# A fused attention and feed-forward layer on one core: where the first stage loads, rounds and stores its weights

## What is computed

```python
xn = _layernorm(x)
q, k, v = xn @ Wq.T, xn @ Wk.T, xn @ Wv.T          # 16 heads of 32
probs = softmax(where(causal, q @ k.T / sqrt(32), min))
attn = (probs @ v) @ Wo.T
gate = silu(xn @ f8(gate_w) * gate_scale)          # 512 x 1536
up = xn @ f8(up_w) * up_scale                      # 512 x 1536
ffn = ((gate * up) @ f8(down_w)) * down_scale      # 1536 x 512
```

## Time and profile before

| | |
|---|---|
| median of 3 runs | 1294.6 us (1293.05 to 1294.61) |
| the profiled execution: time, span | 1293.41 us, 1291.6 us |
| PE busy | 1229.4 us (95%) |
| DVE, ACT, POOL busy | 79%, 71%, 68% |
| granted PE clock, mean | 0.992 |
| end of the first stage | 289.1 us |

### The profile page before, as it was taken

The page is one execution under the profiler, slowest core; times in us unless marked ns, Lnnn a source line. Parts: engine busy times, 40 slices in busy tenths (PEclk is TensorE's granted clock), DMA queues, the critical chain, the costliest instruction groups (busy, mean ns, idle before and its releaser), DMA issues.

```text
span 1291.6 us, 32678 instructions
## 1 busy us (share of the span) xinstructions
PE 1229.4 (95%) x11852; PEld 829.0 (64%) x11852; DVE 1021.0 (79%) x2587; ACT 912.7 (71%) x1555; POOL 877.8 (68%) x1033
## 2 busy tenths in 40 slices
PE   4999888898999999999999999999999999999988
PEld 3444334346777777676767677777777677777763
DVE  7878757677878788888888787878888888878762
ACT  3433333328878788888888788878888888888870
POOL 1323323306777787787888788879788788888882
PEclk9999989998999999999999999999999999999999
DMA  8698999578666465757566576756575866667655
GB/s 257 162 243 246 223 232 269 160 226 213 141 115 143 103 145 97 160 114 164 116 141 131 134 153 133 147 124 156 104 169 115 161 116 151 123 139 152 119 110 130
DMA packets 428463, 201.32 MB, mean 156 GB/s; under 512 B 339344, under 2 KB 396688, under 8 KB 427792
## 3 DMA queue, kind: packets, MB, share of 16 engines
q1 hardware_dynamic: 409312, 179.32, 63.8%
q10 hardware_dynamic: 18992, 19.93, 5.7%
HBM read 76.03 MB, written 44.30 MB: 93 GB/s over the span
## 4 chain that ended last, share of the span: by engine, by line
PE 40%; POOL 15%; ACT 7%; DVE 5%; issue 5%; DMA 4%; SPq 1%; ACTq 0%
PE bank L1650 12%; PE bank L1664 10%; POOL row L1318 7%; PE bank L1626 6%; DMA p_t<-row 4%; PE pair L1588 3%; PE pair L233 3%; POOL fuse L1300 3%; POOL probs L1151 3%; ACT probs L1375 2%; PE pair L1602 2%; PE pair L1672 2%; DVE row_top L1528 2%; ACT fuse L1420 1%; POOL p L1312 1%
## 5 line engine op out<-in xcount | busy, mean ns | idle before, releaser
L1385 ACT ACTIVATE p<-pair,s_exp 128x512 f32<-128x512 f32 (+1 forms) x384 | 243.6, 635 | 147.5 <-PE pair L1588 140.3
L1318 POOL TENSOR_TENSOR row<-row 128x896 f16<-128x896 f32 (+1 forms) x128 | 256.4, 2014 | 9.6 <-ACT row L1399 9.6
L1375 ACT CAST probs<-p 128x512 f16<-128x512 f32 (+1 forms) x384 | 214.8, 559 | 14.3 <-POOL p L1312 12.2
L1151 POOL TENSOR_TENSOR probs<-p,probs 128x512 f16<-128x512 f32 x192 | 221.5, 1157 | 0.2
L1650 PE MATMUL bank<-shared,wg 128*128 128x256 f16 x1536 | 200.0, 273 | 0.0
L1650 PE MATMUL bank<-shared,wu 128*128 128x256 f16 x1536 | 200.0, 273 | 0.0
L1664 PE MATMUL bank<-wd,fuse 128*128 128x512 f16 x768 | 190.6, 378 | 0.8 <-DVE ff_out L1509 0.8
L1528 DVE TENSOR_REDUCE row_top<-pair 128x1 f32<-128x896 f32 (+1 forms) x128 | 147.6, 1153 | 36.6 <-PE pair L1606 36.3
L1312 POOL TENSOR_SCALAR_AFFINE_SELECT p<-p 128x128 f32<-128x128 f32 (+1 forms) x256 | 107.6, 425 | 97.2 <-ACT p L1385 95.8
L1300 POOL TENSOR_TENSOR fuse<-fu,fuse 128x512 f16<-128x512 f32 x96 | 119.1, 1241 | 63.7 <-ACT fuse L1420 63.4
L1650 PEld LDWEIGHTS bank<-shared,wg 128*128 128x128 f16 x1536 | 142.2, 98 | 23.9 <-DMA shared<-xn_parts 0.4
(11 more groups left out here) (164 smaller groups left out, 2139.0 us busy)
## 6 DMA issues: line engine op xcount, KB each, us to landing
q_st<-q_parts SPq DMA_DIRECT2D x192, 64.0 KB, 2.3
k_st<-k_parts SPq DMA_DIRECT2D x192, 64.0 KB, 1.9
v_parts<-res SPq DMA_DIRECT2D x8, 1056.0 KB, 6.6
v_sb<-v_parts SPq DMA_DIRECT2D x64, 132.0 KB, 2.2
xn_parts<-x_t SPq DMA_DIRECT2D x16, 512.0 KB, 6.8
shared<-xn_parts SPq DMA_DIRECT2D x16, 512.0 KB, 4.9
res<-in_L_attn_x SPq DMA_DIRECT2D x16, 512.0 KB, 4.4
out<-shared SPq DMA_DIRECT2D x32, 256.0 KB, 2.6
```

The costliest lines, as they stand in the source:

```text
L1151: ops.tensor_tensor(probs[n % 2][:, LO, at], p32[e % RING][:, 0:UNIT_WIDTH[u]], probs[n % 2][:, HI, at], ALU.subtract).then_inc(signal, 1)
L1318: nc.gpsimd.tensor_tensor(row16[r][:, w:2 * w], row32[r][:, :], row16[r][:, 0:w], ALU.subtract).then_inc(row_lo, 1)
L1375: nc.scalar.copy(probs[n % 2][:, HI, u * 512:u * 512 + w], p32[e % RING][:, 0:w]).then_inc(p_hi, 1)
L1385: nc.scalar.activation(p32[e % RING][:, 0:w], st_bank[u % 2][:, 0:w], ACT.Exp, scale=s_exp[:, :]).then_inc(exp_done, 1)
```

## The change

Everything stands in `prepare`. The loads of raw parts are issued after chunks 7, 8 and 10 in tiles 2 to 5. A part of down_w is 128 columns of half its rows (512-byte pieces) where it was 64 columns of all rows (256-byte pieces). The order of the last parts and all rounding steps move. Heads 0 and 1 have their early maxima in tiles 4 and 5 where they were in tiles 5 and 6. Wo is turned in tile 6 where it was in tile 5. The two kept weights are stored in tile 0 where they were stored in tile 6. The feed-forward bounds move from tile 6's last chunk to tile 7.

```diff
-WEIGHTS_COPIED = {(0, 3): (1,), (0, 6): (2,), (5, 8): (3,)}
+WEIGHTS_COPIED = {(0, 3): (1,), (0, 6): (2,), (6, 3): (3,)}
...
-FF_PARTS = [(i, t) for t in range(NT) for i in range(3)]
+FF_PARTS = [(0, 0), (1, 0), (2, 0), *((i, t) for t in range(1, NT - 2) for i in range(3)),
+            (0, NT - 2), (1, NT - 2), (0, NT - 1), (1, NT - 1), (2, NT - 2), (2, NT - 1)]
...
-            13: ((4, 1), (4, 2), (4, 3)), 14: ((4, 4), (4, 5), (4, 6)), 15: ((4, 7), (4, 8), (4, 9)),
-            16: ((5, 0), (5, 1), (5, 2)), 17: ((5, 3), (5, 4), (5, 5)), 18: ((5, 7), (5, 8), (5, 9)),
...
-            23: ((7, 9), (7, 10), (7, 11))}
-MAXIMA_AT, SPREAD_AT, FACTORS_AT = (6, 11), (7, 8), (7, 9)
-WEIGHTS_KEPT = {(6, 7): 0, (6, 8): 1}
...
+            **{3 * t + i: ((t, 3 * i + 1), (t, 3 * i + 2), (t, 3 * i + 3)) for t in range(2, NT - 2) for i in range(3)},
+            18: ((6, 0), (6, 1), (6, 2)), 19: ((6, 3), (6, 4), (6, 5)), 20: ((6, 5), (6, 6), (6, 7)),
+            21: ((6, 8), (6, 9), (6, 10)), 22: ((7, 9), (7, 9), (7, 10)), 23: ((7, 11), (7, 11), (7, 11))}
+MAXIMA_AT, SPREAD_AT, FACTORS_AT = (7, 8), (7, 10), (7, 10)
+WEIGHTS_KEPT = {(0, 1): 0, (0, 5): 1}
...
-FF_LOADED = {(1, 0): ((0, 1), (1, 1)), (1, 5): ((2, 1),), (1, 7): ((0, 2),), (1, 10): ((1, 2),),
-             **{following(*FF_STEPS[p - 3][2]): (FF_PARTS[p],) for p in range(8, len(FF_PARTS))}}
+FF_LOADED = {(1, 0): (3, 4), (1, 7): (5,), (1, 8): (6,), (1, 10): (7,), (2, 0): (8,),
+             **{(t, c): (3 * t + 3 + i,) for t in range(2, NT - 2) for i, c in enumerate((7, 8, 10))},
+             (NT - 2, 2): (21,), (NT - 2, 8): (22,), (NT - 2, 9): (23,)}
...
+EARLY_TILE = 4
 EARLY_MAXIMA = ({c: (2 * (c - 3), 2 * (c - 3) + 1) for c in range(3, 7)},
-                {c: (2 * (c - 2), 2 * (c - 2) + 1) for c in range(2, 6)})
+                {c: (2 * (c - 4), 2 * (c - 4) + 1) for c in range(4, 8)})
...
-    down_v = down_w.rearrange("(c p) (t o) -> t p c o", p=P, o=DCOL)
+    down_v = down_w.rearrange("(h c p) (t o) -> h t p c o", h=2, p=P, o=DCOL)
...
-                wait(act, rounded, FF_PARTS.index((i, t - 1)) + 1 if t else 0)
+                wait(act, rounded, p - 2)
...
-                        if head == 1 and c == 1:
+                        if head == 1 and c == 2:
                             turn_maxima(nc, pe, rows, bank[7], ident, 0)
```

More of the change, by code:

```diff
@@ L406, in chunk, with raw_part @@
             return (c, c + 4, c - 4)[c // 4] if t == LAST - 1 else c
+        def raw_part(p):
+            return raw[:, p % 3, :] if p % 3 < 2 else raw_down[:, :]
         def has_next(t):
@@ L564, in _ @@
                 norm_factor(t)
-                if t == LAST:
+                if t == EARLY_TILE + 2:
                     low_maxima(nc, pool, rows, 0, 0)
@@ L637, in _ @@
             weights_high(1)
-            for i in range(3):
-                load_ffn_part(i, 0)
+            for p in range(3):
+                load_ffn_part(p)
             def tile(t, par):
@@ L659, in tile @@
                         load_x(X_LOADED[t, c])
-                    for i, r in FF_LOADED.get((t, c), ()):
-                        load_ffn_part(i, r)
+                    for p in FF_LOADED.get((t, c), ()):
+                        load_ffn_part(p)
                     for m in WEIGHTS_SPLIT.get((t, c), ()):
@@ L766, in _ @@
             weights_max(2)
-            def raw_part(i):
-                return raw[:, i, :] if i < 2 else raw_down[:, :]
             def magnitude(p):
                 i, t = FF_PARTS[p]
-                part = raw_part(i)
-                dve.wait_ge(ffw_loaded[i], 16 * (t + 1))
+                part = raw_part(p)
+                dve.wait_ge(ffw_loaded[p % 3], 16 * (p // 3 + 1))
                 if i < 2:
@@ L797, in take_step_off @@
                 dve.wait_ge(round_link, 3 * p + 3)
-                mag, part = cmag[:, :], raw_part(i)
+                mag, part = cmag[:, :], raw_part(p)
                 if i < 2:
@@ L801, in take_step_off @@
                 else:
-                    dst = wd8[:, :, t * DCOL:(t + 1) * DCOL]
-                    mag, part = mag.rearrange("p (c o) -> p c o", c=FC), part.rearrange("p (c o) -> p c o", c=FC)
+                    dst = wd8[:, t // 4 * FC // 2:(t // 4 + 1) * FC // 2, t % 4 * DCOL:(t % 4 + 1) * DCOL]
+                    mag, part = mag.rearrange("p (c o) -> p c o", o=DCOL), part.rearrange("p (c o) -> p c o", o=DCOL)
                 nc.vector.scalar_tensor_tensor(dst, mag, -1.5 * 2.0 ** -99, part, ALU.mult, ALU.add
@@ L912, in tile @@
                             norm_statistics(int(m))
-                    if LAST - 2 <= t < LAST:
-                        head = t - (LAST - 2)
+                    if EARLY_TILE <= t < EARLY_TILE + 2:
+                        head = t - EARLY_TILE
                         if head == 0 and c == min(EARLY_MAXIMA[0]):
@@ L939, in turn_weights @@
                     if m == 3:
-                        pe.wait_ge(rows.m_red, NM)
+                        pe.wait_ge(rows.m_red, 2 * NM)
                     wait(pe, wt_act if n % 2 == 0 else wt_dve, 2 * m + n // 2 - 1)
```

25 lines of the change are left out of this document (13 added, 12 removed), and 6 rows, old and new, of the table FF_STEPS.

## The result

The changed kernel takes 1276.4 us (median of 4 runs, 1274.4 to 1280.5) where the kernel before takes 1294.6 in the same series (1293.05 to 1296.04). The ratio is 0.9864, 95% interval 0.9836 to 0.9891: 1.1 to 1.6% faster. A second series gave 1279.3 us and 0.9897 (0.9866 to 0.9928). By the mean of the two ratios (0.9880) the changed kernel would take 1279.1 of 1294.6, so more than half of these 3.6 us is the spread from series to series. The profiled execution took 1275.57 us (span 1273.7 us).

What follows compares the result with a forecast made beforehand. PE, busy for 95% of the span, was taken as the bound. Tiles 4 to 6 (-14.2) and the stage's end (+2.1) gave -12.1 us on 1293.4, 1281.3; 1.7 for small waits made 1283 us, range 1280 to 1296.

Steps and rivals of the forecast that it cites:

- The load that meets the transposition: Tile 4: moving the up_w load off the high transposition removes the wait for x, 31.3 for 41.7 us, minus 10.4.
- The first rival: Tiles 2 to 5: loads meet the low transposition; one late about 1289 us (chance 0.13), more 1294 to 1309 (0.15).
- The small waits: Tile starts: 1.7 us added for waits like those in tiles 1 and 5 (1.65 and 0.4 us).
- Tile 4: With early maxima moved in: 31.1 + 1.2 for matmuls + 2.4 for waits = 34.7 us, from 41.7.
- Tile 5: New PE waits of 1.3 us (head 0's maxima) and 2.6 us (`m_row` copy), no half clock: 36.3 us, from 38.3.
- the third rival: Tile 5: DVE's lag grows by 2 us, adding 2 + 1.5 us: 1286; inside the 0.55 for 1280 to 1287.
- Tile 6: No maxima there, but the turn of Wo: 31.1 + 1.8 = 32.9 us, from 38.2.
- The edits at nothing: 512-byte pieces of down_w and kept weights stored in tile 0: no cost; late stores could cost tile 1 2 to 3 us.
- The end of the stage: Tile 7: DVE, now with the bounds' maxima and a second part, ends at T+16.5 against 14.4: plus 2.1 us, all on the path.
- The sum stopped at the stage's end: First-stage terms only, -14.2 + 2.1 = -12.1 us; the second stage was forecast at 0.

Runs made afterwards that it cites:

- up_moved: The kernel before with only the up_w loads of tiles 3 and 4 issued after chunk 8 instead of chunk 4; 1280.0 us, ratio 0.9908.
- gate_early: The changed kernel with the gate_w loads of tiles 2 to 5 issued after chunk 4 instead of chunk 7; 1285.6 us, ratio 0.9955.
- after_again: The changed kernel itself, run once more for a second trace and more times; 1279.3 us, ratio 0.9897.
- kept_down_back: The changed kernel with kept weights stored in tile 6 again and down_w parts of 64 columns (256-byte pieces) again; 1278.1 us, ratio 0.9897.

## Why the range was missed, step by step

**The load that meets the transposition: right.** "minus 10.4" for tile 4's wait was 10.7 us for tiles 3 and 4 in up_moved (72.96 to 62.22 us of PE's time). The rule that I weighed (the Trainium skill, "DMA: Bandwidth & Descriptors", "Queues, rings and completion order": each DMA engine takes the queues that have work in turn, a packet at a time) gave, by my estimate, a transposition late by 1 to 2 us. The traces do not agree with that estimate: in gate_early the rate fell to 146 GB/s in the meeting, and both the load of up_w (11.6 us to land, 5.8 in the changed kernel) and the transposition came late. Why most meetings at 0.6 to 1.1 us are bad was not tried.

**The first rival was half real.** Low transpositions did meet loads, in the first trace at 0.41 and 1.21 us, and landed in 7.0 and 7.2 us; in after_again one at 0.96 us needed 11.1 us and cost 1.8. Less than half a microsecond of issue time lies between a clean tile and a late one.

**The small waits: the first step that failed.** I added 1.7 us for waits at tile starts "of the kind seen in tiles 1 and 5". They did not come, and a wait of 0.6 us for DVE in tile 2 of before went too. This is 2.6 of the 7.5 us by which the first pair of traces passes the forecast. Without this term the forecast, 12.1 us, is close to what the first stage gave on the mean of four traces (12.5).

**Tile 4: mis-sized by 1.1 us.** I gave the waits for DVE 2.4 us; one of 0.96 us was left.

**Tile 5: right by luck in the first trace.** The waits were 1.03 and 2.86 for the forecast 1.3 and 2.6. The second was not worked out rightly: the terms given, 14.3 + 0.6 + 1.5 + 0.2, make T+16.6 and not T+16.9, so 2.3 us of waiting, and with the 2.6 used the tile's terms add up to 36.4 and not 36.3. A second error covered this one. The low half of chunk 2 started at T+14.1, but the "add" behind it took 2.3 us, not the 1.5 that I had read from the last part at the stage's end (DVE, timeline of the changed kernel):

```profile
203.66 0.56 DVE L782 TENSOR_SCALAR res<-res 128x768 f32<-128x768 f32 x1
204.26 1.79 DVE L785 SCALAR_TENSOR_TENSOR raw<-res,raw 128x768 f32<-128x768 f32 x1
205.97 0.20 DVE L285 COPY m_row<-bank 12x128 f16<-12x128 f16 x1
```

And "neither is as long as 3.9, so I count no half clock" was wrong in three of four traces, where 3.4 us of half clock follow and tile 5 takes 38.0 to 38.3 for my 36.3: it is the half clock of the third rival, at a shorter wait than I gave it. On the typical trace the move of the maxima gains nothing in tile 5; its gain is tile 6, less what tile 4 takes on.

**Tile 6: right** (32.87 for 32.9). **The edits at nothing: right** within what the times can show, with the low transposition of tile 1 as an open end (kept_down_back).

**The end of the stage: right in size, wrong in what it costs.** DVE's last operation ended at T+16.9 for 16.5, the stage 2.4 us later for 2.1. But I took "all of it on the path". Of these 2.4 us 1.5 come back, since DVE now works behind the last low half and the store of v is 3.3 us old when the second stage issues its loads.

**The sum stopped at the stage's end: the step that failed most.** I let the second stage stand at nothing because its code is the same. It lasted 4.4 us less in the first pair and 2.6 on the mean of four; 1.5 are the store of v, and the rest lies within the spread of 4 us from trace to trace in the unchanged code, its cause open. My lower bound lay 3 us under the forecast and left no room for either. That the first series came out at 1276.4 and not at the 1279.1 of the mean ratio is luck; even that is 0.9 us below the range.

## What to carry to other kernels

Look at when two queues' transfers start, not only at how many bytes they move: a load issued 0.6 to 1.1 us behind a DMA transposition doubled its time in most cases, and two issue places moved by four chunks gave 12 of the 13 to 18 us. Then look whether the meeting is paid at all: in the kernel before, two late transpositions cost PE 9 us for tile 4 and two more 0.4 us for tile 5, because tile 4 was late already. Where a stage ends with all engines together, work that is put behind its last store lets the store drain, and part of its price comes back at the next stage's first loads. A sum over a stage needs a range for the rest of the kernel too, from two traces of the same kernel if there are two.

## What was not expected of the hardware

- A transposition from one queue and a 384 KB load from another, issued 0.64 to 0.78 us apart, took twice their time in 12 of 14 cases. In two windows inside such meetings (before, gate_early) the DMA engines' busy share was 1.2 and the rate 84 and 146 GB/s; in one where they met 1.2 us apart it was 266.
- Issuing a load took 1.2 us instead of 0.47 on ACT's queue when a store of v (1056 KB, SP's queue) had been issued 1.5 and 2.8 us before, though it is another queue; with the store issued 3.6 us before or more it did not.
- A wait of 2.86 us came with 3.4 us at the lower clock level (1.2 GHz), begun within 0.7 us of its end, in three of four traces of the changed kernel and with none in the fourth; over all traces with this wait, in seven of nine. The wait of 3.8 us in tile 6 came with 3.4 or 6.8 us of it in the four traces of the kernel before and with none in up_moved; a wait of 0.27 us with none.
